# Layer 1's first key operands in other buffers, a wait moved into the first expert tile, and the up copies begun two pieces later

## The reference

```python
x = x + tanh(g_xattn[0]) * xattn0(layernorm(x), ctx, ctx)   # 16 heads of 16
x = x + tanh(g_ffn[0])   * experts(layernorm(x))            # 8 experts, 2 for each token
x = x + tanh(g_xattn[1]) * xattn1(layernorm(x), ctx, ctx)   # the same with biases
x = x + tanh(g_ffn[1])   * gated(layernorm(x))

# experts, on the first 1024 tokens' slots sorted by expert:
h = gelu(xs @ w1[e]); ys = h @ w2[e]; out[tok] += ys * weight
# gated, each act_qdq with one scale for the whole tensor (max |value| / 32767):
up = act_qdq(x @ w_up.T);  gate = act_qdq(x @ w_gate.T)
gate = act_qdq(gate * fixed16(sigmoid(gate)));  out = act_qdq(gate * up) @ w_down.T
```

## Time and profile before

| what | us |
|---|---|
| median of three runs | 872.63 (872.58, 872.63, 874.93) |
| the profiled execution, its own time | 875.18 |
| its span, first to last instruction | 873.2 |
| PE busy | 806.9 |
| DVE busy | 639.4 |
| ACT busy | 554.3 |
| POOL busy | 216.6 |

### The profile page before, as it was taken

The page is one execution under the profiler, slowest core; times in us unless marked ns, Lnnn a source line. Parts: engine busy times, 40 slices in busy tenths (PEclk is TensorE's granted clock), DMA queues, the critical chain, the costliest instruction groups (busy, mean ns, idle before and its releaser), DMA issues.

```text
span 873.2 us, 15450 instructions
## 1 busy us (share of the span) xinstructions
PE 806.9 (92%) x4898; PEld 483.9 (55%) x4899; DVE 639.4 (73%) x1222; ACT 554.3 (63%) x743; POOL 216.6 (25%) x344
## 2 busy tenths in 40 slices
PE   9999999999997999999898999999999969992198
PEld 6543333333356999999864433333333557881198
DVE  5898888888777232225268978888888388988975
ACT  4557777777765444444245667777777677496985
POOL 3342111573052331001071523000003608100000
PEclk9999999999999999999999999999999989996599
DMA  8898476663025555654389653443320000000002
GB/s 292 178 272 252 98 181 171 148 172 99 2 95 176 193 182 185 215 200 181 126 265 263 196 179 76 87 88 80 75 62 2 0 1 1 1 1 0 0 25 73
DMA packets 67569, 106.90 MB, mean 122 GB/s; under 512 B 24374, under 2 KB 46774, under 8 KB 67510
## 3 DMA queue, kind: packets, MB, share of 16 engines
q1 hardware_dynamic: 55580, 65.73, 29.0%
q0 software_dynamic: 10208, 37.75, 13.0%
q10 hardware_dynamic: 1728, 2.75, 0.9%
HBM read 78.37 MB, written 27.44 MB: 121 GB/s over the span
## 4 chain that ended last, share of the span: by engine, by line
PE 77%; DVE 10%; ACT 7%; issue 3%; DMA 2%; SPq 1%; POOL 0%; DVEq 0%; ACTq 0%; POOLq 0%
PE PS L2361 14%; PE PS L2329 13%; PE PS L2350 12%; PE PS L2508 9%; PE PS L2524 5%; PE PS L2461 3%; PE PS L2529 3%; PE PS L2602 2%; PE PS L2275 2%; PE PS L2292 2%; PE PS L2312 2%; PE PS L2375 2%; PE PS L2630 1%; PE PS L2635 1%; PE PS L2639 1%
## 5 line engine op out<-in xcount | busy, mean ns | idle before, releaser
L1708 DVE TENSOR_REDUCE MX<-PS 128x1 f32<-128x512 f32 x512 | 320.9, 682 | 44.2 <-PE PS L2329 43.6
L1258 ACT ACTIVATE Pt<-PS 128x1024 f32<-128x1024 f32 x256 | 248.1, 1021 | 100.9 <-PE PS L2350 100.9
L2329 PE MATMUL PS<-KSt,BIG 96*128 96x512 bf16 x512 | 175.8, 384 | 3.5 <-DVE bias_row L1595 2.7
L2350 PE MATMUL PS<-BIG,KSt 99*128 99x512 bf16 x512 | 150.1, 379 | 2.0 <-ACT Pt L1258 1.4
L2361 PE MATMUL PS<-Pt,VS 128*17 128x512 f32 x1024 | 137.1, 601 | 0.0
L2329 PEld LDWEIGHTS PS<-KSt,BIG 96*128 96x128 bf16 x512 | 40.4, 97 | 144.4 <-DVE MX L1708 88.0
L2508 PE MATMUL PS<-KSt,Pt 128*128 128x128 f32 x736 | 87.7, 278 | 2.3 <-issue 2.3
L2508 PEld LDWEIGHTS PS<-KSt,Pt 128*128 128x128 f32 x736 | 85.8, 195 | 2.7 <-issue 2.7
L2350 PEld LDWEIGHTS PS<-BIG,KSt 99*128 99x128 bf16 x512 | 49.5, 98 | 56.0 <-ACT Pt L1258 4.8
L1820 DVE COPY KSt<-PS 128x256 f32<-128x256 f32 x23 | 9.7, 424 | 94.2 <-PE PS L2492 94.2
L896 POOL TENSOR_TENSOR MP<-MX,zrow 128x16 bf16<-128x16 f32 x32 | 7.0, 220 | 250.0 <-DVE MX L1708 250.0
(11 more groups left out here) (221 smaller groups left out, 1324.7 us busy)
## 6 DMA issues: line engine op xcount, KB each, us to landing
Pt<-in_w POOLq DMA_DIRECT2D x21, 1024.0 KB, 5.3
qk_parts<-BIG SPq DMA_DIRECT2D x64, 192.0 KB, 3.3
W<-in_w POOLq DMA_DIRECT2D x8, 1024.0 KB, 6.7
BIG<-qk_parts SPq DMA_DIRECT2D x32, 192.0 KB, 3.3
KSt<-qk_parts SPq DMA_DIRECT2D x32, 192.0 KB, 3.8
v_rows<-BIG SPq DMA_DIRECT2D x8, 544.0 KB, 4.3
VS<-v_rows SPq DMA_DIRECT2D x32, 136.0 KB, 3.5
BIG<-qk_parts SPq DMA_DIRECT2D x32, 128.0 KB, 3.9
```

The source lines that it names most:

```text
L1258: act.activation(PP[:, 2 * (kc % 2) + half, :, :].rearrange("p h t -> p (h t)"), ST[half], ACT.Exp, scale=DK ** -0.5).then_inc(exp_done, 1)
L1708: dve.tensor_reduce(MX[:, g % 2, i % TB, i // TB:i // TB + 1], ring(i), AX.X, ALU.max, negate=True).then_inc(max_taken, 1)
L2329: pe.matmul(ring(i), QS[0:ROWS, g, h, qc * P:(qc + 1) * P], KS[0:ROWS, g, h, :], start=True, stop=True).then_inc(max_done, 1)
L2350: last = pe.matmul(ST[half][:, i * S:(i + 1) * S], KS[0:ROWS + PARTS, g, h, kc * P:(kc + 1) * P], QS[0:ROWS + PARTS, g, h, :], start=True, ...
```

## The change

Three edits that do not touch each other.

1. Layer 1's key weight goes to `TT` and the context of its first batch to the first quarter of `Pt`. SP loads the key weight as soon as attention 0's last output is projected (`out_done` 16), and the context when the last tile's `hidden` is done (`h_done` 46). The value weight is then the first transfer behind the last `y`, ahead of the last store; the rest follows in the old order. PE makes all four key steps of the first batch before its first three value tiles (before: one key step, two value tiles, a key step, a value tile, two key steps). ACT copies both blocks of turned tokens ahead of the middle parts and takes the two halves of the first values later; DVE makes the second low part before the third rest and the first `combine`.
2. The two waits for `w2` move from ahead of `expert_tile(0, 0, 0)` into it, behind `hidden` of tile 1 and the transposes of tile 2, right ahead of the `y` product.
3. ACT copies up pair 0 in piece 3 instead of piece 1, and so on to pair 8 in piece 11. DVE takes the maxima of pairs 0, 1, 2 straight from PSUM (two before piece 0, one in piece 2), of pairs 3 to 7 at the start of pieces 6 to 10, of 8 and 9 in piece 11, of 10 in piece 12, and of 11 between the two small reductions.

```diff
         def context(layer, p):
+            if layer and p == 0:
+                return Pt[:, 0:KC * S].rearrange("p (c t) -> p c t", c=KC)
...
         def weight(layer, which):
+            if layer and which == 1:
+                return TT[:, :, :]
...
-        PAIRS_SOON = 2
+        PAIRS_SOON = 3
+        COPY_AT = 3
+        def maxima_at(i):
+            if i == 0:
+                return range(2)
+            if i == 2:
+                return range(2, 3)
+            if COPY_AT + PAIRS_SOON <= i < PIECES - 1:
+                return range(i - COPY_AT, i - COPY_AT + 1)
+            return {PIECES - 1: range(PIECES - 4, PIECES - 2), PIECES: range(PIECES - 2, PIECES - 1)}.get(i, ())
...
@@ SP @@
             sp.dma_start(WO[:, :, :], io["attn_w"][1, 3]).then_inc(wo_in, 16)
+            load_weight(sp, 1, 1, awk_in)
...
             for t in range(SLOT_TILES - 3, SLOT_TILES):
+                if t == SLOT_TILES - 2:
+                    sp.wait_ge(h_done, 2 * SLOT_TILES)
+                    load_context(sp, 1, 0)
                 if t == SLOT_TILES - 1:
                     sp.wait_ge(y_done, SLOT_TILES)
-                    load_weight(sp, 1, 1, awk_in)
-                    load_context(sp, 1, 0)
+                    load_weight(sp, 1, 2, awv_in)
                 store_results(t // 2, t % 2)
-            load_weight(sp, 1, 2, awv_in)
@@ ACT, prep_second @@
-                take_half(1, 0, 0)
                 high_part(1, "k", 0, 0)
+                copy_xnt(1, 0, 0)
                 middle_part(1, "k", 0, 0)
                 high_part(1, "k", 0, 1)
-                copy_xnt(1, 0, 0)
+                copy_xnt(1, 0, 1)
                 middle_part(1, "k", 0, 1)
+                take_half(1, 0, 0)
+                high_part(1, "k", 1, 0)
                 take_half(1, 0, 1)
-                high_part(1, "k", 1, 0)
-                copy_xnt(1, 0, 1)
                 middle_part(1, "k", 1, 0)
@@ ACT, gated @@
-                if 1 <= i <= UP_KEPT:
-                    copy_pair(i - 1)
+                if COPY_AT <= i < COPY_AT + UP_KEPT:
+                    copy_pair(i - COPY_AT)
@@ DVE, prep_second @@
                 rest_of(1, "k", 0, 1)
+                low_part(1, "k", 0, 1)
+                rest_of(1, "k", 1, 0)
                 combine(0)
-                rest_of(1, "k", 1, 0)
-                low_part(1, "k", 0, 1)
                 combine(1)
@@ DVE, gated @@
-            for j in range(PAIRS_SOON):
-                pair_max(j).then_inc(up_maxed, 1)
             for i in range(PIECES + 1):
+                for j in maxima_at(i):
+                    last = pair_max(j)
+                    if j < PAIRS_SOON:
+                        last.then_inc(up_maxed, 1)
                 dve.wait_ge(sig_done, i + 1)
                 dve.tensor_scalar(steps_piece(i), sig_piece(i), SIG_STEPS, None, ALU.mult).then_inc(sig_round, 1)
-                if i > PAIRS_SOON:
-                    pair_max(i - 1)
                 product(i)
...
             dve.tensor_reduce(cm[:, 0:1], cmx[:, 32:33 + PIECES], AX.X, ALU.max).then_inc(col_max, 1)
+            link(dve, pair_max(PIECES - 1))
             dve.tensor_reduce(cm[:, 1:2], cmx[:, 0:PIECES], AX.X, ALU.max).then_inc(col_max, 1)
@@ PE, prep_second @@
                 key_step(1, 0, 0, 0)
-                pe.wait_ge(awv_in, 32)
-                value_steps(1, 0, range(2))
                 key_step(1, 0, 0, 1)
-                value_steps(1, 0, range(2, 3))
                 key_step(1, 0, 1, 0)
                 key_step(1, 0, 1, 1)
+                pe.wait_ge(awv_in, 32)
+                value_steps(1, 0, range(3))
@@ PE, experts @@
                     turn_slots(m, q, 2)
+                if t == 0:
+                    pe.wait_ge(w2_early, EARLY_EXPERTS * FC * D // 512)
+                    pe.wait_ge(w2_low, len(W2_LATE))
                 pe.wait_ge(h_high, 2 * n + 2)
...
-            pe.wait_ge(w2_early, EARLY_EXPERTS * FC * D // 512)
-            pe.wait_ge(w2_low, len(W2_LATE))
             expert_tile(0, 0, 0)
```

## The result

The changed kernel takes 867.61 us (867.01 to 869.79, 6 runs), beside 873.17 us (872.58 to 875.37) for the kernel before in the same session. The ratio is 0.9928 with a 95% interval of 0.9916 to 0.9941: 6.3 us less (5.2 to 7.3), where 7.9 were forecast. (The two medians are 5.6 us apart; where this text says what a kernel gained, it goes by the ratio.) It is faster by more than the 0.3% that can be told from no change; the median lies 2.9 us above the forecast and 0.1 above the upper end of its range, though the kernel before was 0.5 slower beside it than its 872.63 ahead of the forecast: the ratio times that 872.63 gives 866.3, inside the range. The profiled execution took 868.87 us with a span of 866.8, 6.4 less than the span before.

What follows compares the result with a forecast made beforehand. PE, busy 92% of the span, bounds it through idle time and low clock at the expert stage's ends; ACT and DVE bound the gated stage. 3.3 + 3.5 + 1.1 = 7.9 us less gives 864.7 us, range 862.5 to 867.5.

Steps and rivals of the forecast that it cites:

- The wait for `w2`: Start of the expert stage: moving the wait behind tile 1's `hidden` gains 3.3 us, bounds 1.6 and 3.7.
- It starts at about 278.2 and, without a gap, keeps the clock: 3.74 us: Expert stage: tile 1's `hidden` on PE starts at about 278.2 and takes 3.74 us instead of 5.43.
- does not move: Expert stage: tile 0's `hidden`, which sets POOL's issue of tile 2's `w1` at 279.85, keeps its time.
- The key operands: Between the experts and attention 1: early key weight and context with new orders gain 3.5 us.
- its 5.5 less 2.1: Keys and values on PE: idle time 3.87 and slow clock 1.6 won, two new stalls take back 2.1 us.
- The up copies: Gated stage: later copies and moved maxima on ACT and DVE gain 1.1 us, bounds 0 and 1.4.
- So DVE is 0.9 better off: Gated stage, early pieces: DVE's idle time of 3.7 us shrinks to 2.8.
- the up copies give nothing: Rival, gated stage: DVE's idle time only moves to pieces 3 to 5; 865.8 us, chance 0.09.
- tile 1 gets little faster: Rival, expert stage: clock down despite the closed gap, or next `w1` late; 1.6 us from this edit, 866.4, chance 0.08.
- The clock in the new stall: Rival: clock falls in PE's stall ahead of the third value tile, costing 1.3 us; 866.0, chance 0.17.
- The slower loop of attention 1: Rival: loop entered in another phase to SP's stack loads, PE losing 10.5 us of 155; chance 0.02.
- The term without a sign: DVE's product at 467.58 beside POOL's low parts: shifted lists change the sum by up to 1.8 us either way; taken as 0.

Runs made afterwards that it cites:

- e_w2: The kernel before with only the two waits for `w2` moved: 871.41 us against 874.24, ratio 0.9969.
- after: The changed kernel with all three edits, in its profiled execution of 868.87 us: ratio of the timed runs to the kernel before 0.9928.
- e_keys: The kernel before with only the key operands' buffers, early loads and new orders of PE, ACT and DVE: 870.87 us, ratio 0.9967.
- up_between: The changed kernel with, from piece 6 on, each piece's maximum between its steps and product again: 876.41 us beside 883.4 for the kernel before, ratio 0.992.

## Why the prediction was right or wrong

**The two gaps and the last maximum** were the right places. The three parts alone give 2.7, 2.9 and 0.7 us, together 6.3, the whole change's 6.3. With 1.1 us of uncertainty on each of these numbers that is partly luck: it only says that the parts don't disturb each other by several us.

**The wait for `w2`: forecast 3.3, measured 2.7 (1.6 to 3.8) alone; stretch A shrinks by 1.8 where neither execution has a fall.** The step that failed is "It starts at about 278.2 and, without a gap, keeps the clock: 3.74 us", with its premise that tile 0's `hidden` "does not move". In e_w2 both hold. In the changed kernel's own execution tile 0's `hidden` takes some 5.3 instead of 3.7 us, so tile 1's comes later by that, though it keeps the clock. I read 5.43 us behind a gap of 2.12 as the gap's sure price; but the clock falls in some executions and not in others, in both kernels, so part of the 1.7 is no gain, and where the clock falls in tile 0 the old wait had hidden it. How the 1.7 is shared out in the timed medians isn't shown, since no kernel was profiled more than twice. The forecast's 3.5 for the first `y` is what a fallen execution of before against an unfallen one of after shows (A: 14.29 to 10.74, 3.55). The Trainium skill ("TensorE: Matmul & The Clock Gate", Part 1) says that the activity is sampled on a beat of its own that doesn't start with the kernel, so that the transition moves with where the work falls in it; that fits the traces: with 0.90 and 0.56 us of idle time ahead of tile 0 in after, and 0.89 and 0.57 in e_w2, the clock fell in the one and not in the other. The second small error: `w1` of tile 2 was to cost 0.2, and at clock 1.0 the distance from the first `y` to tile 2's `hidden` grew from 2.95 (e_keys) to 3.39 (e_w2), 0.44.

**The key operands: forecast 3.5, measured 2.9 (1.7 to 4.0).** The sum was right within what can be measured, with its parts (its 5.5 less 2.1 is 3.4, not the 3.6 that came from the list of times; a slip that changes nothing): keys without idle time, stalls of 1.45 and 0.41 for 1.5 and 0.6, 3.5 less to the first query step for 3.6, the rest of k(2,0) 3.5 nearer to the turned blocks than before (24.55 us behind them instead of 28.05) for 3.5, the clock at 1.0 behind the stall. Two things I didn't see. The kernel before's own B of 18.81 is the shortest of four, so more is gained there on other executions, and the gathers take some of it back in one of them (1.20). And I never priced the new order against the old one with early operands: it is 1 us worse at the first query step.

**The up copies: forecast 1.1, measured 0.71, of which 0.67 is the last maximum.** The step that failed is "So DVE is 0.9 better off". The last product of the changed kernel starts at 791.45, 36.84 us after the first pair maximum. In the kernel before, timeline, DVE, these two are
```profile
760.26 1.22 DVE L1988 TENSOR_REDUCE cmx<-PS 128x1 f32<-128x1024 f32 x1
...
798.17 1.21 DVE L1997 CUSTOM_DVE_ANT_0 BIG<-BIG 128x1024 f32<-128x1024 uint16 x1
```
and 37.91 apart. Of the 1.07 between them the maximum that went behind the product is 1.13, so the early pieces gave nothing. DVE has no idle time from 770.46 on, and there a piece takes 3.00 us, with the maximum ahead of the steps, where it takes 2.88 in up_between's order when it waits for nothing (0.61, 1.12 and 1.15). The list that forecast the last product's end 37.54 us after the first maximum (797.8 - 760.26) left that 0.1 a piece out; it is 38.07. Over the seven pieces from 770.46 on that is 0.8 us (7 times 0.12), an estimate, and enough for the 0.53 that is missing. The rival "the up copies give nothing" was right about the idle time and wrong in its total, since the last maximum brings its gain without it.

**The other rivals.** For the rival that tile 1 gets little faster, the changed kernel's profile shows the price (A 1.80 less than before), but at another place: the clock is down in tile 0. The clock in the new stall: not there, B is 15.31 or 15.32 in all six executions with that order. The slower loop of attention 1: from the first exponential to the first pair maximum it takes 260.50 before and 260.57 after, and 259.0 to 260.6 in all fourteen executions. The term without a sign came out as 0 in this pair of traces; timeline of the changed kernel, DVE:
```profile
461.60 1.11 DVE L1524 TENSOR_TENSOR nw<-nw,ve 128x8 f32<-128x8 f32 x1
```
It is 1.11 again, beside POOL's low parts as in the earlier trace rows, while in e_keys another instruction is hit (the 1.07 at 462.95 above).

## What to carry to other kernels

Before a low clock is priced as the result of a gap, look at several executions, of sibling kernels too: what comes and goes in either kernel is no sure gain, however near to the gap it stands. And a wait that is removed can have been the cover of something else: here the wait for `w2` hid a fall of the clock ahead of it. An edit of several parts wants each part priced against the kernel that has the others; here two moved lines carry the up copies, and early loads without the new order bring as much as with it. On an in-order engine an operation that doesn't need a wait's data belongs ahead of that wait: it cost 0.1 us a piece in lost overlap and filled 1.03 us of idle time.

## What the runs showed of the hardware

The granted clock fell to 0.50 inside tile 0's `hidden` in five of the twelve executions without extra fillers, behind idle pieces that add up to 1.46 to 1.56 us, and not in the other seven with 1.35 to 1.49; at the end of a gap of 2.1 us it fell in two of four; behind the stall of 1.45 us in stretch B, which follows PE's unbroken work, in none of six.

Two chips ran the same kernel before in 883 to 885 us where the first took 874, with ACT standing up to 10.6 us in one stretch of the changed kernel, by the code for a store to land; the ratio of changed to before agrees on both kinds within the intervals (0.9928 and 0.9912). A gain on the path beside such a stretch can't be measured there, though those further away can. And on DVE the product, which reads what the steps ahead of it wrote and waits for their semaphore, starts 0.71 us after them, where an independent maximum of the same length in its place starts after 0.61. Whether the 0.1 is the price of the data or of the semaphore wasn't tried.
